# Transposes of the row maxima moved behind the first quarter of the late out-product, in a cross-attention and FFN block

## Chip, core and metric
The kernel runs on one core of one Trainium2 chip. The metric is the device time of one execution in microseconds (us). An execution has five engines that run their own instruction streams and meet by semaphores: TensorE (PE, with PEld for its weight loads), VectorE (DVE), ScalarE (ACT), GpSimd (POOL) and SyncE (SP), which issues the DMAs.

## What is computed
x is 4 x 2048 rows of 512, the context 4 x 154 rows of 512. Both residual branches have a layer norm ahead of them.

```python
x = x + _L0_xattn_ref(_layernorm(x), ctx, ctx, Wq, Wk, Wv, Wo, lam, g)
x = x + _L0_ffn_ref(_layernorm(x), ln1_g, ln1_b, w1, b1, ln2_g, ln2_b, w2, b2)
# attention: 16 heads of 32, two sets of queries and keys, 8 key heads
w1 = softmax(q1 @ k1.T); w2 = softmax(q2 @ k2.T)
attn = (w1 - lam * w2) @ v                     # then RMS norm, scale g, @ Wo.T
# ffn: 512 -> 2048 -> 512, weights quantised to -1, 0, 1 times a step
h = gelu(layer_norm(x, ln1_g, ln1_b) @ w1q.T + b1)
out = layer_norm(h, ln2_g, ln2_b) @ w2q.T + b2
```

## The kernel before, in words
The 8192 rows are cut into 16 blocks of 512 (`NBLK`), each of four groups of 128 rows (`tt`, 0 to 3). Weights, their transposes and the keys of the context are made once, in `setup` and `PROLOGUE`. Products in near-float32 precision are made of two or three float16 products of a high and a low part.

Every engine has a function `iteration(i)`, and the order of the work is written out by hand. There is no planner. The list `ATTEND` gives the first part of a block for all engines as words: `s` scores, `v` values, `q` a query product of the next block, `a` a piece of the attention result, and for the block before `e`, `f`, `h`, `i` parts of its late out-product, `g` the sums over its gelus, `y` and `z` the additions that finish its rows.

```python
ATTEND = [... "e2 g f2 y0 y1 s0 q0 z0 z1 y2 s1 v0 s2 h3 v1 ..." ...]
```

A block has these stages. In the first part (`ATTEND`) PE makes scores and values for block i, and finishes what the block before left. Then come the output projection (`out_projection`, L1173 to L1175 called with woT), the RMS sums, the rest of the queries, and a chain over DVE, ACT and POOL (`normalise`, `mid_rows`, layer norm) until PE transposes the normalised rows (`h_transposes`, L1315). The last stage is the FFN: 16 steps j. In each step PE makes the hidden product (`hidden`, L1325), scores of block i+1 in rows (`row_scores`, L1225), of which DVE takes the maxima (`row_max`, L890), and the out-product of the groups 0 and 1 three steps behind (`ffn_step`, L1347, PSUM banks 2 and 3). ACT makes gelu (L680, L683, L685), DVE the low part (`gelu_lo`, L987), and POOL sums the gelus and their squares (`sum_gelu`, L526). The out-product of the groups 2 and 3 is "late": it is made in the next block by `ffn_late` (L1337), group 2 in bank 5, as `e2` (four of 16 steps, eight matmuls) and `f2` (twelve steps, 24 matmuls), with `g` (`gelu_sums`, L1358, into bank 4) between them.

The row maxima of block i+1 are needed as two more rows of the operand `stack`, from which the scores of that block are made. When the last of 44 maxima is taken, DVE splits them (`split_maxima`, L897, L898, L900, semaphore `negmax_lo`), PE transposes them in four transposes into bank 6 (`transpose_maxima`, L1232, `negmax_transposed`), DVE copies them to SBUF (`copy_maxima`, L906), and SP brings them to `stack` in two DMAs (`stack_maxima`, L433, `negmax_stacked`). The first scores of a block (`scores`, L1250) write banks 0 to 3 and wait for three things around the change:

```python
wait(pe, s_nmst, c, 32, 32)        # the two DMAs of the maxima
wait(pe, s_gln, c - 1, 1, 1)       # L1001, which read the sums in bank 4
wait(pe, s_y, c - 1, TT, 2)        # y0, y1: add_ffn has read banks 2 and 3
```

`y0` and `y1` are `add_ffn` (L1013) on DVE. They need the scale of the layer norm over the gelus: `gelu_norm` on DVE (L994, L996, L998, L1001), a power on POOL (`power`, L483), then L1003 and L1005 on DVE. On POOL the four additions of a constant (`add_constant`, L513) stand ahead of that power, and they follow the last `sum_gelu`.

Of the kernel before, what the change touches and what calls it, by code (L numbers as in the profile page):

```python
# [91 lines left out]
def maxima_beside(j):  # L92

    first = sum(MAXIMA_AT[:j])
    return list(range(first, first + MAXIMA_AT[j]))


def wait(eng, sem, c, per, k):

    if isinstance(c, int) and c * per + k <= 0:  # L100
        return
    eng.wait_ge(sem, c * per + k)


def build(nc, x, ctx, wq, wk, wv, wo, lam, g, ln1_g, ln1_b, w1, b1, ln2_g, ln2_b, w2, b2, out):
# [7 lines left out]
    with ExitStack() as es:  # L113
# [17 lines left out]
        def ffn_bank(tt):  # L131

            return 2 + tt if tt < 2 else B_Q
# [950 lines left out]
        def _(pe):  # L1084
# [144 lines left out]
            def transpose_maxima(c):  # L1229
                wait(pe, s_nmlo, c, 1, 1)  # L1230
                for tt in range(TT):
                    ins = pe.transpose(ps[:, B_O, 0:TB // 2].bitcast(F16)[:, tt * P:(tt + 1) * P],  # L1232
                                       negmax16[:, tt, :, :].rearrange("p e u -> p (e u)"), ident16[:])
                ins.then_inc(s_nmt, 1)

            def scores(c, gi):


                if gi == 0:
                    wait(pe, s_nmst, c, 32, 32)  # L1240
                    if c:
                        wait(pe, s_gln, c - 1, 1, 1)
                        wait(pe, s_y, c - 1, TT, 2)
                    if c < NBLK - 1:
                        wait(pe, s_xt_lo, c + 1, TT, TT)
                else:
                    wait(pe, s_p, c, 2 * QM, 2 * gi)
                for i in range(UPT):
                    u = UPT * gi + i
                    ins = pe.matmul(ps[:, i, :], k_att[0:STKM, key_unit(u), 0:P], stack[0:STKM, u, :], start=True, stop=True)  # L1250
                    if i == 1:
                        ins.then_inc(s_s, 1)
                for i in range(UPT):
                    u = UPT * gi + i
                    ins = pe.matmul(ps[DH * i:DH * i + DH, B_SREST, :], k_att[0:STKM, key_unit(u), P:SPAD],  # L1255
                                    stack[0:STKM, u, :], start=True, stop=True)
                ins.then_inc(s_s, 1)

            def values(c, gi):

                m, buf = ORDER[gi] % (QM // 2), gi % 2
                b_o, b_l = value_banks(gi)
                wait(pe, s_p, c, 2 * QM, 2 * gi + 2)
                if gi == 0:
                    pe.wait_ge(s_vatt, 16 * (c // BLK_PER_BATCH + 1))
                elif gi % 2 and gi < QM - 1:
                    wait(pe, s_ol1, c, KD, gi // 2 + 1)
                else:
                    wait(pe, s_o2, c, KD, gi // 2)
                for i in range(UPT):  # L1270
                    kv = (UPT * m + i) // (H // KV)
                    pe.matmul(ps[DH * i:DH * i + DH, b_o, :], v_att[:, kv * DH:(kv + 1) * DH], probs[:, buf, i, :],  # L1272
                              start=True, stop=False)
                if gi % 2 == 0 and gi > 0:
                    wait(pe, s_ol2, c, KD, gi // 2)
                if gi == 0 and c < NBLK - 1:
                    wait(pe, s_q32, c + 1, QM, 1)
                for i in range(UPT):
                    pe.matmul(ps[DH * i:DH * i + DH, b_l, :], ones[:, 0:DH], probs[:, buf, i, :], start=True, stop=False)  # L1279

                wait(pe, s_r_lo, c, QM, gi + 1)
                v_hi, v_lo = (v_att[:, VM:].bitcast(F16).rearrange("p (h n) -> p h n", h=2)[:, h, m * P:(m + 1) * P]
                              for h in range(2))
                split_product(ps[:, b_o, :], v_hi, v_lo, p16[:, buf, 0, :], p16[:, buf, 1, :], False, True)
                pe.matmul(ps[:, b_l, :], ones_rest[:], p16[:, buf, 0, :], start=False, stop=False)
                pe.matmul(ps[:, b_l, :], ones_rest[:], p16[:, buf, 1, :], start=False, stop=True).then_inc(s_pv, 1)
# [9 lines left out]
            def out_projection(c, tt, pairs):  # L1296

                wait(pe, s_att_lo, c, KD, pairs[-1] + 1)
                cols = slice(tt * P, (tt + 1) * P)
                for k in pairs:  # L1300
                    ins = split_product(ps[:, tt, :], attn16[:, 0, k, cols], attn16[:, 1, k, cols], woT_hi[:, k, :],
                                        woT_lo[:, k, :], k == 0, k == KD - 1)
                if pairs[-1] == KD - 1:
                    ins.then_inc(s_wo, 1)
# [24 lines left out]
            def ffn_late(c, tt, js):  # L1329

                for j in js:
                    if j == 0 and tt == 2:
                        wait(pe, s_gelu, c, JH, JH)
                    elif j == 0:
                        wait(pe, s_y, c, TT, tt)
                    for e in range(2):
                        ins = pe.matmul(ps[:, ffn_bank(tt), :], gg16[:, j, e, tt * P:(tt + 1) * P], w2T[:, j, :],  # L1337
                                        start=(j == 0 and e == 0), stop=(j == JH - 1 and e == 1))
                if js[-1] == JH - 1:
                    ins.then_inc(s_f2, 1)  # L1340
# [11 lines left out]
            def gelu_sums(c):  # L1352

                wait(pe, s_acc, c, JH - 1, JH - 1)
                wait(pe, s_gelu, c, JH, JH - 1)
                for e in range(2):
                    for tt in range(TT):
                        ins = pe.matmul(ps[:, B_H, e * TT + tt:e * TT + tt + 1], acc[:, e, tt * P:(tt + 1) * P],  # L1358
                                        ones[:, 0:1], start=True, stop=True)
                ins.then_inc(s_sums, 1)  # L1360

            def iteration(i):
                ahead, ahead2 = i < NBLK - 1, i < NBLK - 2
                for what, n in ATTEND:
                    if what == "s":
                        scores(i, n)
                    elif what == "v":
                        values(i, n)
                    elif what == "e" and i:
                        ffn_late(i - 1, n, range(JH // 4))  # L1370
                    elif what == "f" and i:
                        ffn_late(i - 1, n, range(JH // 4, JH))
                    elif what == "h" and i:
                        ffn_late(i - 1, n, range(JH // 2))
                    elif what == "i" and i:
                        ffn_late(i - 1, n, range(JH // 2, JH))
                    elif what == "g" and i:
                        gelu_sums(i - 1)
                    elif what == "q" and ahead:
                        queries(i + 1, n)  # L1380
                for tt in range(TT):
                    if tt == TT - 1:
                        wait(pe, s_ol2, i, KD, KD)
                    out_projection(i, tt, (0, 1, 2))
                out_projection(i, 0, (3,))
                out_projection(i, 1, (3,))
                rms_sums(i)
                out_projection(i, 2, (3,))
                out_projection(i, 3, (3,))
                if ahead:  # L1390
                    for n in range(QATT, QEARLY):
                        queries(i + 1, n)
                h_transposes(i)
                if ahead:
                    for n in range(QEARLY, QM):
                        queries(i + 1, n)
                banks = (2, 3) if ahead else range(TT)
                for j in range(JH):
                    beside = maxima_beside(j) if ahead else []
                    hidden(i, j)  # L1400
                    for tb in beside[:2]:
                        row_scores(i + 1, tb)
                    if j >= FLAG:
                        ffn_step(i, j - FLAG, banks)
                    for tb in beside[2:]:
                        row_scores(i + 1, tb)
                    if ahead2 and j in XT_AT:
                        x_transposes(i + 2, XT_AT[j])
                for j in range(JH - FLAG, JH):
                    ffn_step(i, j, banks)  # L1410
                if ahead:
                    transpose_maxima(i + 1)

            setup()
            for what, n in PROLOGUE:
# [50 lines left out]
```

## Time and profile before

| | |
|---|---|
| median of 3 runs | 2459.5 us (2456.2 to 2461.03) |
| the profiled execution | 2460.22 us |
| its span, first to last instruction | 2456.9 us |
| mean granted clock of TensorE | 0.973 |
| busy: PE, DVE, ACT, POOL | 2301.5, 1719.6, 1339.5, 1012.2 us |

The profile is one execution. All places in time are us from the start of its span. Engine names with a q are their sequencers (SPq issues DMAs). Matmuls are pipelined: one of 512 columns is shown 0.38 us long, while the next may start after 0.22. "Idle before" is counted from the modelled end of the last one. A releaser is the instruction whose semaphore ended the wait.

### The profile page before, as it was taken

To read this page: it belongs to the slowest core of one execution; us is meant where nothing else is said; L and a number is where in the kernel's file an instruction comes from. 1 tells how busy PE (TensorE), PEld (TensorE's weight loads), DVE (VectorE), ACT (ScalarE), POOL (GpSimd) and SP (SyncE) were. 2 spreads that over 40 slices of the span, in tenths; PEclk is the share of its full clock that TensorE was granted. 3 is DMA by queue.
4 is the path that set the end of the run, shared out by engine and by line. 5 is a ranking of instruction groups with operands and counts; after the bars stand their busy time and mean duration, and the time that the engine had idled before them with its cause. 6 is when DMAs were issued, how large, how long until landed. Compare 5 with 4: busy or idle time off the path is not lost.

```text
span 2456.9 us, 35564 instructions
## 1 busy us (share of the span) xinstructions
PE 2301.5 (94%) x13663; PEld 1082.5 (44%) x13663; DVE 1719.6 (70%) x2714; ACT 1339.5 (55%) x1943; POOL 1012.2 (41%) x823
## 2 busy tenths in 40 slices
PE   8488999999999999999999999999999999999978
PEld 5243444535344453535444353534445353544433
DVE  3865858678585868768586776858586785857563
ACT  3325555546555555556555555655555465555544
POOL 0220543617153452716345271625436172534517
PEclk9688999999999999999999999999999999999989
DMA  6220203021130302111030202103030211202000
GB/s 256 74 77 11 69 15 89 13 69 26 37 84 15 90 15 68 25 60 44 23 97 15 78 15 69 36 23 82 15 101 19 65 27 33 72 15 74 15 22 17
DMA packets 105643, 125.85 MB, mean 51 GB/s; under 512 B 22496, under 2 KB 74268, under 8 KB 104964
## 3 DMA queue, kind: packets, MB, share of 16 engines
q1 hardware_dynamic: 105476, 123.60, 17.4%
q8 instruction: 108, 1.77, 0.3%
q14 instruction: 59, 0.48, 0.1%
HBM read 51.80 MB, written 20.36 MB: 29 GB/s over the span
## 4 chain that ended last, share of the span: by engine, by line
PE 69%; DVE 19%; issue 3%; ACT 3%; POOL 3%; DMA 2%; SPq 1%; POOLq 0%; ACTq 0%; DVEq 0%
PE ps L1325 16%; PE ps L1337 9%; PE ps L1347 7%; PE ps L1272 5%; PE ps L1225 5%; PE ps L1250 4%; PE ps L1173 4%; PE ps L1279 4%; PE ps L1174 3%; PE ps L1175 3%; DVE attn_raw L928 2%; DVE arena L987 2%; DVE arena L876 2%; DVE arena L890 2%; PE ps L1255 2%
## 5 line engine op out<-in xcount | busy, mean ns | idle before, releaser
L526 POOL TENSOR_TENSOR attn_raw<-attn_raw 128x512 f32<-128x512 f32 x448 | 580.2, 1314 | 146.5 <-ACT attn_raw L685 138.7
L1325 PE MATMUL ps<-rows,w1T 128*128 128x512 f16 x2048 | 485.5, 380 | 24.1 <-DVE rows L982 24.1
L890 DVE TENSOR_REDUCE arena<-ps 128x3 f32<-128x462 f32 (+1 forms) x704 | 413.8, 619 | 96.5 <-PE ps L1225 95.4
L494 POOL TENSOR_TENSOR q<-q 128x512 f16<-128x512 f32 x128 | 155.9, 1222 | 695.3 <-ACT q L631 678.5
L680 ACT ACTIVATE attn_raw<-ps,vec_cols,wstep 128x512 f32<-128x512 f32 x256 | 198.6, 776 | 267.0 <-PE ps L1325 265.2
L987 DVE SCALAR_TENSOR_TENSOR arena<-attn_raw,vec_cols,arena 128x512 f16<-128x512 f32 x256 | 233.1, 911 | 84.7 <-ACT arena L683 83.2
L1325 PEld LDWEIGHTS ps<-rows,w1T 128*128 128x128 f16 x2048 | 191.0, 97 | 220.7 <-DVE rows L982 37.2
L651 ACT ACTIVATE arena<-ps 128x1024 f32<-128x1024 f32 x128 | 131.6, 1028 | 266.6 <-PE ps L1250 266.6
L1347 PE MATMUL ps<-w2T,arena 128*128 128x512 f16 x1088 | 271.1, 379 | 0.0
L910 DVE SCALAR_TENSOR_TENSOR p<-arena,p 128x512 f16<-128x512 f32 x128 | 88.1, 689 | 254.4 <-ACT p L655 254.4
L1225 PE MATMUL ps<-k_att,stack_raw 96*128 96x154 f16 x2048 | 223.2, 234 | 23.1 <-DVE arena L890 21.6
L1225 PEld LDWEIGHTS ps<-k_att,stack_raw 96*128 96x128 f16 x2048 | 164.2, 98 | 144.4 <-DVE arena L890 66.4
L1337 PE MATMUL ps<-w2T,arena 128*128 128x512 f16 x960 | 217.3, 379 | 0.0
L928 DVE RECIPROCAL attn_raw<-attn_raw 128x512 f32<-128x512 f32 x64 | 214.1, 3346 | 0.0
L1173 PE MATMUL ps<-arena,wqT_hi 128*128 128x512 f16 x512 | 197.9, 387 | 4.7 <-DVE arena L951 4.2
L1174 PE MATMUL ps<-arena,wqT_hi 128*128 128x512 f16 x512 | 197.2, 385 | 0.0
L1175 PE MATMUL ps<-arena,wqT_lo 128*128 128x512 f16 x512 | 196.7, 384 | 0.0
L683 ACT ACTIVATE arena<-attn_raw,vec_cols 128x512 f16<-128x512 f32 x256 | 184.8, 722 | 8.3
L653 ACT ACTIVATE arena<-ps 128x1536 f32<-128x1536 f32 x128 | 186.2, 1455 | 0.4 <-PE ps L1255 0.4
L629 ACT ACTIVATE q<-ps 128x512 f32<-128x512 f32 x128 | 76.4, 596 | 200.8 <-PE ps L1175 180.8
L685 ACT ACTIVATE attn_raw<-attn_raw 128x512 f32<-128x512 f32 x256 | 156.9, 613 | 0.0
L1272 PE MATMUL ps<-arena,v_att 128*32 128x512 f32 x1024 | 136.7, 606 | 2.2 <-ACT arena L651 1.1
(164 smaller groups left out, 3436.5 us busy)
## 6 DMA issues: line engine op xcount, KB each, us to landing
stack_raw<-q SPq DMA_DIRECT2D x768, 64.0 KB, 2.0
arena<-in_x SPq DMA_DIRECT2D x16, 1024.0 KB, 6.2
arena<-in_x SPq DMA_DIRECT2D x64, 256.0 KB, 2.6
out<-arena SPq DMA_DIRECT2D x64, 256.0 KB, 2.0
arena<-in_L_ffn_w SPq DMA_DIRECT2D x8, 1024.0 KB, 10.5
stack_raw<-in_L_xattn_Wq SPq DMA_DIRECT2D x8, 256.0 KB, 10.8
k_att<-k_store SPq DMA_DIRECT2D x4, 490.0 KB
k_store<-attn_raw SPq DMA_DIRECT2D x12, 160.0 KB
```

The lines of the kernel that those rows point to most:

```text
L526: ins = pool.tensor_tensor(acc[:, e, :], acc[:, e, :], src[:, j % NG, :], ALU.add)
L890: dve.tensor_reduce(negmax[:, tt, u0:u1], ps[:, row_bank(c, tb), 0:(u1 - u0) * S].rearrange("p (u s) -> p u s", s=S), AX.X, ALU.max, negat ...
L928: dve.reciprocal(l_prod, l_prod).then_inc(s_inv, 1)
L987: dve.scalar_tensor_tensor(gg16[:, j, 1, :], gelu_t[:, j % NG, :], g2_col[:, j:j + 1], gg16[:, j, 0, :], ALU.mult, ALU.subtract).then_inc( ...
L1173: pe.matmul(dst, w_hi, r_hi, start=first, stop=False)
L1174: pe.matmul(dst, w_hi, r_lo, start=False, stop=False)
L1175: return pe.matmul(dst, w_lo, r_hi, start=False, stop=last)
L1225: ins = pe.matmul(ps[:, row_bank(c, tb), w * S:(w + 1) * S], stack[0:STK, u, tt * P:(tt + 1) * P], k_att[0:STK, key_unit(u), 0:S], start=T ...
L1272: pe.matmul(ps[DH * i:DH * i + DH, b_o, :], v_att[:, kv * DH:(kv + 1) * DH], probs[:, buf, i, :], start=True, stop=False)
L1325: ins = pe.matmul(ps[:, B_H + j % 2, :], w1T[:, k, j * P:(j + 1) * P], rows16[:, e, k, :], start=(k == 0 and e == 0), stop=(k == KD - 1 an ...
L1337: ins = pe.matmul(ps[:, ffn_bank(tt), :], gg16[:, j, e, tt * P:(tt + 1) * P], w2T[:, j, :], start=(j == 0 and e == 0), stop=(j == JH - 1 a ...
L1347: ins = pe.matmul(ps[:, bank, :], gg16[:, j, e, tt * P:(tt + 1) * P], w2T[:, j, :], start=(j == 0 and e == 0), stop=(j == JH - 1 and e == 1))
```

## The change
In `iteration(i)` of PE the call of `transpose_maxima` moves from the end of the block, where it stood for block i+1, to the next block, behind the word `e`. There it is called for block i itself. The call for block 0, ahead of the loop, stays.

```diff
                     elif what == "e" and i:
                         ffn_late(i - 1, n, range(JH // 4))
+                        transpose_maxima(i)
                     elif what == "f" and i:
...
                 for j in range(JH - FLAG, JH):
                     ffn_step(i, j, banks)
-                if ahead:
-                    transpose_maxima(i + 1)
```

On PE the seam between two blocks then reads differently. This is one of the 15 seams, which are all alike. Words in brackets are the semaphores that the instruction waits for (`gelu` the activation, `gelu_summed` POOL's sums, `gelu_lo` DVE's low part).

Before:

```order
L1347 MATMUL ps<-w2T,arena 128x512 x3
L1232 MATMUL ps<-ident,arena 128x128 [waits negmax_lo]
L1232 MATMUL ps<-ident,arena 128x128 x3
L1337 MATMUL ps<-w2T,arena 128x512 [waits gelu]
L1337 MATMUL ps<-w2T,arena 128x512 x7
L1358 MATMUL ps<-ones,attn_raw 128x1 [waits gelu,gelu_summed]
L1358 MATMUL ps<-ones,attn_raw 128x1 x7
L1337 MATMUL ps<-w2T,arena 128x512 x24
L1250 MATMUL ps<-stack_raw,k_att 128x512 [waits ffn_out_read,x_lo,gelu_ln_step,negmax_stacked]
```

With the change:

```order
L1347 MATMUL ps<-w2T,arena 128x512 x3
L1337 MATMUL ps<-w2T,arena 128x512 [waits gelu]
L1337 MATMUL ps<-w2T,arena 128x512 x7
L1232 MATMUL ps<-ident,arena 128x128 [waits negmax_lo]
L1232 MATMUL ps<-ident,arena 128x128 x3
L1358 MATMUL ps<-ones,attn_raw 128x1 [waits gelu,gelu_summed]
L1358 MATMUL ps<-ones,attn_raw 128x1 x7
L1337 MATMUL ps<-w2T,arena 128x512 x24
L1250 MATMUL ps<-stack_raw,k_att 128x512 [waits ffn_out_read,x_lo,gelu_ln_step,negmax_stacked]
```

The four transposes and the eight matmuls of the quarter have changed places, and everything around them stands as before. DVE's part of the seam is the same in both:

```order
L900 SCALAR_TENSOR_TENSOR arena<-arena 128x4x32 [waits negmax_hi]
L906 COPY sq_acc<-ps 64x512 [waits negmax_stacked,negmax_transposed]
L994 TENSOR_SCALAR mean_g<-ps 128x4 [waits gelu_sums]
L996 TENSOR_TENSOR meansq_g<-mean_g 128x4 [waits gelu_ln_small_step]
L998 SCALAR_TENSOR_TENSOR var_g<-ps,meansq_g 128x4 [waits gelu_ln_small_step]
L1001 TENSOR_SCALAR var<-var_g 128x4 [waits gelu_ln_small_step]
L1003 TENSOR_SCALAR scale_g<-rstd,wstep 128x4 [waits gelu_rstd]
L1005 SCALAR_TENSOR_TENSOR shift_g<-mean_g,scale_g 128x4 [waits gelu_ln_small_step]
L1013 SCALAR_TENSOR_TENSOR arena<-ps,scale_g,arena 128x512 [waits gelu_ln_small_step,const_added,ffn_out]
```

Nothing moved here, nor on SP, ACT and POOL; L906 waits for the transposes that moved on PE.

## Rows read from the trace of the kernel before

**Rows 1.** The page: PE's busy time, and the chain that ended last by engine.
```profile
PE 2301.5 (94%) x13663; PEld 1082.5 (44%) x13663; DVE 1719.6 (70%) x2714; ACT 1339.5 (55%) x1943; POOL 1012.2 (41%) x823
...
PE 69%; DVE 19%; issue 3%; ACT 3%; POOL 3%; DMA 2%; SPq 1%; POOLq 0%; ACTq 0%; DVEq 0%
```

**Rows 2.** Waits of PE, 290 to 2300: us in total, times, longest.
```profile
PE ps L1325 <- DVE rows L982: 20.3, 14, 1.6
PE ps L1232 <- DVE arena L900: 14.7, 14, 1.1
```

**Rows 3.** Chain of waits across one seam, 465 to 486: start, us, what.
```profile
466.94 0.79 ACT attn_raw L680
...
471.81 0.40 PE ps L1232 x4
```

**Rows 4.** Timeline of PE at that seam: start, us, what, idle before it.
```profile
468.01 2.75 PE L1347 MATMUL ps<-w2T,arena 128*128 128x512 f16 x12
471.81 0.40 PE L1232 MATMUL ps<-ident,arena 128*128 128x128 f16 x4 [1.05 <-DVE arena L900]
472.05 1.89 PE L1337 MATMUL ps<-w2T,arena 128*128 128x512 f16 x8
473.77 1.84 PE L1358 MATMUL ps<-ones,attn_raw 128*128 128x1 f32 x16
475.48 5.34 PE L1337 MATMUL ps<-w2T,arena 128*128 128x512 f16 x24
480.65 1.03 PE L1250 MATMUL ps<-stack_raw,k_att 98*128 98x512 f16 x4
```

**Rows 5.** Chain of waits in the middle of a block, 526 to 562.
```profile
532.38 0.23 PE ps L1286
...
558.14 1.92 PE ps L1325 x8
```

**Rows 6.** Weight loads: one group of the page, and the timeline at the seam.
```profile
L1325 PEld LDWEIGHTS ps<-rows,w1T 128*128 128x128 f16 x2048 | 191.0, 97 | 220.7 <-DVE rows L982 37.2
...
475.37 4.95 PEld L1337 LDWEIGHTS ps<-w2T,arena 128*128 128x128 f16 x24
```

**Rows 7.** Timeline of DVE at the seam.
```profile
470.50 1.25 DVE L900 SCALAR_TENSOR_TENSOR arena<-arena 128x128 f16<-128x128 f32 x1
472.25 0.42 DVE L906 COPY sq_acc<-ps 64x512 f16<-64x512 f16 x1 [0.49 <-PE ps L1232]
475.65 0.16 DVE L994 TENSOR_SCALAR mean_g<-ps 128x4 f32<-128x4 f32 x1 [2.99 <-PE ps L1358]
...
478.49 1.41 DVE L1013 SCALAR_TENSOR_TENSOR arena<-ps,scale_g,arena 128x512 f32<-128x512 f32 x2
```

**Rows 8.** Timeline of POOL at the seam.
```profile
469.07 2.54 POOL L526 TENSOR_TENSOR attn_raw<-attn_raw 128x512 f32<-128x512 f32 x2 [0.59 <-ACT attn_raw L685]
471.56 4.98 POOL L513 TENSOR_TENSOR arena<-arena,out_const 128x512 f32<-128x512 f32 x4
477.05 1.02 POOL L483 TENSOR_TENSOR rstd<-var,neghalf 128x4 f32<-128x4 f32 x1 [0.50 <-DVE var L1001]
```

**Rows 9.** Timeline of POOL in mid-block: two powers in a row.
```profile
543.88 2.00 POOL L483 TENSOR_TENSOR rstd<-var,neghalf 128x4 f32<-128x4 f32 x2 [2.00 <-DVE var L942]
```

**Rows 10.** SP's two DMAs at the seam, and the landing of all 32.
```profile
472.69 1.20 SPq L433 DMA_DIRECT2D stack_raw<-sq_acc  x2
...
DMA to landing us min/median/max: 2.7/3.3/3.7
```

**Rows 11.** Busy us (and instructions) by stretch: PE, PEld, DVE, ACT, POOL, PEclk, DMA, GB/s.
```profile
330.00:470.70 140.70, 136.64 (x821) 63.63 (x820) 102.22 (x159) 80.84 (x116) 61.89 (x51) 1.00 0.17 46
...
689.85:693.26 3.41, 3.38 (x9) 1.17 (x10) 3.33 (x9) 0.31 (x1) 1.11 (x2) 0.50 0.45 108
```

**Rows 12.** Timeline of PE in block 3, a query product.
```profile
689.88 0.59 PE L1173 MATMUL ps<-arena,wqT_hi 128*128 128x512 f16 x1 [2.24 <-DVE arena L951]
...
693.25 0.39 PE L1175 MATMUL ps<-arena,wqT_lo 128*128 128x512 f16 x1
```

## The prediction
> **What bounds the kernel now.** I read the engine shares on the page, then TensorE's waits in the steady part, then the chain of waits, and last the timelines of every engine around one seam between two blocks. PE is busy 94% of the span, and the chain that ended last lies on PE for 69% and on DVE for 19% [rows 1]. So a wait of PE is paid in full unless something else is just as late. In the steady part the two longest waits of PE [rows 2] are L1325, after the projection's layer norm, and L1232, the transposes of this change: 14.7 us in 14 places, never over 1.1 us. The chain of waits across the seam [rows 3] goes back from the transposes to the last gelu on ACT. It is a latency chain of ACT and DVE that PE waits out.
>
> The timelines of the seam between blocks 1 and 2 [rows 4] give the size. Late out-product matmuls start 0.216 us apart (24 of them last 5.34 with the last taking 0.38: 4.96 / 23). The last matmul of the early out-product starts at 468.01 + 2.75 - 0.38 = 470.38, so PE could issue the next at 470.60. It issues the first transpose at 471.81, released by DVE's L900 of 470.50 + 1.25 = 471.75. **The hole is 471.81 - 470.60 = 1.21 us**; the view calls 1.05 of it idle, because it counts from a modelled end. The hole stands in front of each of 15 transposes in the loop. In the other 14 seams the distance from L900 to L1232 looks the same, since the longest of these waits is 1.1.
>
> Everything else in a block hangs on PE. In the middle of a block the chain leaves PE's last value product (L1286), runs over DVE, ACT and POOL, and comes back to PE at L1325 [rows 5]. It starts from PE and has no fixed time of its own. What PE gains at the seam should therefore stay gained to the end.
>
> **The change, step by step.** It adds and removes nothing: four transposes move past the eight matmuls of `ffn_late(i - 1, 2, first quarter)` on PE. The instructions of DVE, SP, POOL and ACT keep their order, so no queue but PE's is passed.
>
> 1. The quarter moves up. It waits for the last gelu, which ends at 466.94 + 0.79 = 467.73 [rows 3], 2.9 us before 470.60. It starts at 470.60 and takes 473.77 - 472.05 = 1.72 [rows 4], until 472.32. Cost nothing; it fills the hole.
> 2. The transposes now come up at 472.32. Their data is there at 471.75 [rows 7], and 0.06 later PE was released before, so the wait is covered with 0.51 us to spare. They take 472.05 - 471.81 = 0.24. PE goes on at 472.56. If the cover were gone (data over 0.5 us later), the rest of the wait would simply come back.
> 3. The weight load of the first transpose now stands behind a running matmul. A load takes 97 ns, and the 24 loads of the late product lie within 4.95 us beside 24 matmuls 0.216 us apart [rows 6], so a load of this size hides. I take 0, upper bound 0.10 per seam. The Trainium skill's page "TensorE: Matmul & The Clock Gate" (Part 3, The mechanism) says that a weight load overlaps running matmuls only when it goes to another row group. The late product's loads and matmuls use the same 128 rows, so by that rule each pair would stand 0.31 us apart; the trace disagrees.
> 4. The sums (`gelu_sums`, L1358) come at 472.56 instead of 473.77, 1.21 earlier. They wait for POOL's last sum of gelus, which ends at 469.07 + 2.54 = 471.61 [rows 8]: 0.95 us to spare. The 24 matmuls behind them are issued 1.21 earlier too. PE is ready for the scores (L1250) at 480.65 - 1.21 = 479.44.
> 5. The scores wait for two things that do not move by 1.21, and here the change can lose.
>    - **The second `add_ffn`** (L1013), which frees the last of the banks that the scores write, ended at 478.49 + 1.41 = 479.90 [rows 7], 0.75 before the scores. Its chain starts with the sums: L994 to L1001 on DVE, the power on POOL, L1003, L1005, two L1013. DVE's part moves by 1.21: L1001, which released the power at 477.05, now could at 475.84. But POOL is in its four additions until 471.56 + 4.98 = 476.54, and these do not move. So the power starts at 476.54 and not at 477.05 [rows 8], 0.51 earlier, and L1013 ends at 479.39. A release of 0.05 or 0.06 behind that makes 479.45, against PE's 479.44. I take 0.01 us lost. Whether POOL starts the power right behind an addition is not seen at this place; where two powers follow each other they last 2.00 us together against 1.02 for one [rows 9], which leaves no pause. Bounds: the chain moves by 0.55 (nothing lost), or not at all (scores at 479.95, 0.51 lost).
>    - **The maxima's copy and DMA.** DVE's copy L906 follows the transposes, from 472.25 to 472.77. SP issues two DMAs in a row (1.20 us together), landing at most 3.7 us after issue [rows 10]. Before, SP started 0.02 after the copy, so now at 473.21; the second issue is at about 473.82 and lands by 477.5. That is 1.9 us ahead of 479.44. Cost nothing. DVE's copy also stands ahead of L994, which starts at 474.4 at the earliest; the copy ends at 473.2.
>
> Sum: 15 seams x 1.21 = 18.2 us gained, 15 x 0.01 = 0.2 lost, 18.0 net. The profiled execution took 2460.2 us (span 2456.9 and 3.3 around it), the median of the runs is 2459.5, 0.7 lower. So 2442.2 for an execution like the profiled one, and **2441.5 for the median**. That is 0.73%, where a measurement of this kernel can tell about 0.2% (4.9 us) from no change.
>
> **Rivals.**
> (a) *POOL and the add hold the scores.* The hole is closed but a part of it opens again in front of L1250, because POOL's power comes late behind the additions, or because L1013 is slower beside them. At worst the scores stand at 479.95: 1.21 - 0.51 = 0.70 per seam, 10.5 us, 2449.0. For it: the margin is only 0.01 us. Against it: POOL shows no pause between operations. Chance 0.09.
> (b) *The moved loads do not hide.* One load of 0.10 exposed per seam: 1.5 us less gain, 2443.0. The rows against it are in step 3. This is what the quoted rule of the Trainium skill would do here. Chance 0.02.
> (c) *The maxima land late.* The copy ends 0.52 later and the scores are wanted 1.21 earlier, so slack shrinks by 1.73. If a DMA needed twice its time (6.6 instead of 3.3), it would land at 480.4, the scores would start 0.2 earlier than before, and the time would be 2457, no change that can be told. Against it: 3.7 is the longest of 32 landings [rows 10], and nothing else uses the queue then. Chance 0.04.
> (d) *The clock, slower than before.* PE's clock is at its full level (1.00, 2.4 GHz) through the ordinary blocks, and at 0.50 (1.2 GHz) in a stretch of block 3 [rows 11]. That stretch begins where PE had stood idle for 2.24 us in front of a query product [rows 12], and there eight matmuls stood 0.42 instead of 0.216 us apart, which costs 1.6 us. PE also idles 1.5 us in front of L1325 in each block. If the new spacing of blocks made the clock fall there each time, it would cost 15 x 1.6 = 24.7 us, 6.5 more than the gain: 2466. It turns the sign from 11 blocks on. Against it: the 1.05 us of idle time that goes stood in stretches at 1.00, and less idle time is no reason for a lower clock. A dip more or less (1.6 us) is likely enough and belongs to the range. Chance 0.03.
> That the change does not do what it says is excluded by the order of PE's instructions.
>
> **How the numbers follow.** My forecast has 0.82, (a) 0.09, (b) 0.02, (c) 0.04, (d) 0.03. The forecast, (a) and (b) are faster: 0.93; (c) is no change: 0.04; (d) is slower: 0.03. The low end takes the lowest run before, 2456.2, less the full 18.2: 2438.0. The high end is the bound of (a), 2449.0. (c) and (d) are left out, with the tails of the rest.
>
> **What would show it.** In the new profile the seam should read, on PE: L1347, L1337 x8, L1232, L1358 without idle time between them, and L1232 gone from the waits. From L1347's last start to L1250's first there should be 9.06 us instead of 10.27 in all 15 seams. POOL's power should follow the additions at once, with DVE as no releaser, and L1250 should have next to no wait. The ordinary block should take about 139.5 us instead of 140.7 (the length of the first stretch in [rows 11]). It would be wrong if L1250 showed a wait on L1013 of over 0.2 us (rival a), if a gap opened at L1232's load (b), if L1250 waited for the DMA (c), or if the granted clock fell in many blocks (d), and wrong in its premise if PE's seam were 1.2 us shorter and the block as long as before.

## The result, and the profile after

| | before | changed |
|---|---|---|
| first comparison, median | 2460.01 us (4 runs) | 2443.55 us (4 runs, 2443.25 to 2449.02) |
| second comparison, median | 2459.1 us (9 runs) | 2446.17 us (5 runs, 2443.27 to 2448.67) |
| profiled execution, span | 2456.9 us | 2446.6 us |

The change makes the kernel faster. The ratio was 0.9941 (95% interval 0.9924 to 0.9959) the first time and 0.9945 (0.9932 to 0.9959) the second. That is 10 to 19 us and 10 to 17 us. I had forecast 18.0 us, 2441.5 us.

One execution differs from another by several us for reasons outside the change (shown further down). The seams are a sharper measure, because the ordinary block repeats to a few hundredths. It took 140.7 us before [rows 11]. In the changed kernel a stretch of 139.77 us holds the same 821 matmuls (columns as there):

```profile
471.00:610.77 139.77, 136.66 (x821) 63.63 (x820) 102.97 (x158) 80.85 (x116) 61.89 (x51) 1.00 0.17 46
```

So a seam gives 0.92 us (140.69 from one L900 to the next before, 139.77 now) and 15 seams give 13.8 us. The forecast was 1.20 per seam.

Waits of PE from 290 to 2300 us in the changed kernel (us in total, times, longest):

```profile
PE ps L1325 <- DVE rows L982: 20.5, 14, 1.9
PE ps L1225 <- DVE arena L890: 13.2, 28, 0.6
...
PE ps L1250 <- issue: 0.4, 2, 0.2
```

The transposes' wait (L1232, 14.7 us in [rows 2]) is gone and the others stand as before. PE's timeline at the same seam answers to [rows 4]:

```profile
467.13 2.75 PE L1347 MATMUL ps<-w2T,arena 128*128 128x512 f16 x12
469.72 1.89 PE L1337 MATMUL ps<-w2T,arena 128*128 128x512 f16 x8
471.45 0.39 PE L1232 MATMUL ps<-ident,arena 128*128 128x128 f16 x4
471.67 1.90 PE L1358 MATMUL ps<-ones,attn_raw 128*128 128x1 f32 x16
473.43 5.34 PE L1337 MATMUL ps<-w2T,arena 128*128 128x512 f16 x24
478.87 1.02 PE L1250 MATMUL ps<-stack_raw,k_att 98*128 98x512 f16 x4
```

I count from the start of the last L1347 matmul, 467.13 + 2.75 - 0.38 = 469.50. The hole in front of the transposes has closed. The last late matmul starts at 473.43 + 5.34 - 0.38 = 478.39, so PE could take the scores at 478.61, 9.11 behind the mark. L1250 starts at 478.87, 9.37 behind it; before it was 10.27. A new hole of 0.26 us has opened, too short for the view to print as idle. DVE and POOL at the seam, answering to [rows 7] and [rows 8]:

```profile
473.61 0.16 DVE L994 TENSOR_SCALAR mean_g<-ps 128x4 f32<-128x4 f32 x1 [1.32 <-PE ps L1358]
473.80 0.66 DVE L996 TENSOR_TENSOR meansq_g<-mean_g 128x4 f32<-128x4 f32 x1
474.50 0.16 DVE L998 SCALAR_TENSOR_TENSOR var_g<-ps,meansq_g 128x4 f32<-128x4 f32 x1
474.69 1.00 DVE L1001 TENSOR_SCALAR var<-var_g 128x4 f32<-128x4 f32 x1
...
477.20 1.41 DVE L1013 SCALAR_TENSOR_TENSOR arena<-ps,scale_g,arena 128x512 f32<-128x512 f32 x2
```

```profile
470.69 4.97 POOL L513 TENSOR_TENSOR arena<-arena,out_const 128x512 f32<-128x512 f32 x4
475.77 1.02 POOL L483 TENSOR_TENSOR rstd<-var,neghalf 128x4 f32<-128x4 f32 x1
```

Two of the rows that [rows 7] leaves out, from the same timeline of the kernel before:

```profile
475.85 0.72 DVE L996 TENSOR_TENSOR meansq_g<-mean_g 128x4 f32<-128x4 f32 x1
...
476.80 0.17 DVE L1001 TENSOR_SCALAR var<-var_g 128x4 f32<-128x4 f32 x1
```

L1001 works on four numbers per partition. It took 0.17 us before and now takes 1.00. It ends at 475.69, 0.03 behind the end of POOL's four additions (475.66). `add_ffn` (L1013) ends at 477.20 + 1.41 = 478.61, and L1250 follows 0.26 behind that.

**The rest of the profiled execution.** Its time, 2449.02 us, is 5.5 above the other three runs of the first comparison. DVE's timeline in block 4 shows one cause:

```profile
822.17 2.47 DVE L861 BATCH_NORM_STATS2 stats<-arena 128x6 f32<-128x512 f32 x4 [2.06 <-DMA arena<-in_x]
```

The 1 MB load of x landed 10.0 us after its issue there and 9.8 in block 10; the median of the loads is 6.2. Those two blocks took 141.93 and 141.72 us instead of 139.77. The order of the loads did not change, and the second profile of the changed kernel has 139.78 us in block 4 and 139.79 in block 10. So this is scatter that the change did not bring. (A third load, in block 11, took 9.97 us; there PE's granted clock also stood at 0.50 for 3.4 us, from 1812.9 on, behind 2.15 us of idle time in front of a query product.)

The mean granted clock goes with the scatter between executions. Of the 39 executions of the kernel before that stood beside the experiments, 16 had 0.973 or 0.974 (median 2461.7 us) and 8 had 0.977 or more (2457.6 us). Of the nine executions of the changed kernel, five had 0.973 or 0.974 (2446.4 us) and four 0.977 or more (2443.4 us); three of these four stand in the first comparison. At like clocks the difference is 15.2 and 14.2 us. One difference of the clock lies in the setup, which the change does not touch. From 17.5 to 27.7 us the clock stood at 0.50 in the profile of the changed kernel and at 1.00 in that of experiment 1, though PE had the same 19 matmuls in both.

### The profile page after: what moved, and what is told of

The parts are those of the page before. It is cut to its first block, busy times and chain, and to the rows that moved or that the text cites. A ratio compares the mean times of both kernels' runs of the same rounds, so it can differ in the third digit from the quotient of the medians.

```text
span 2446.6 us, 35564 instructions
## 1 busy us (share of the span) xinstructions
PE 2303.2 (94%) x13663; PEld 1082.0 (44%) x13663; DVE 1731.0 (71%) x2714; ACT 1340.0 (55%) x1943; POOL 1011.9 (41%) x823
## 4 chain that ended last, share of the span: by engine, by line
PE 70%; DVE 17%; issue 3%; DMA 3%; POOL 3%; ACT 2%; SPq 1%; POOLq 0%; ACTq 0%; DVEq 0%
PE ps L1325 16%; PE ps L1347 9%; PE ps L1337 9%; PE ps L1225 5%; PE ps L1272 5%; PE ps L1250 4%; PE ps L1173 4%; PE ps L1279 4%; PE ps L1174 3%; PE ps L1175 3%; DVE attn_raw L928 2%; DVE arena L987 2%; DVE arena L876 2%; PE ps L1255 2%; DMA arena<-in_x 2%
## 5 line engine op out<-in xcount | busy, mean ns | idle before, releaser
L987 DVE SCALAR_TENSOR_TENSOR arena<-attn_raw,vec_cols,arena 128x512 f16<-128x512 f32 x256 | 233.2, 911 | 85.1 <-ACT arena L683 83.5
L1347 PE MATMUL ps<-w2T,arena 128*128 128x512 f16 x1088 | 271.1, 379 | 0.0
L1337 PEld LDWEIGHTS ps<-w2T,arena 128*128 128x128 f16 x960 | 91.6, 99 | 109.5 <-issue 6.8
## 6 DMA issues: line engine op xcount, KB each, us to landing
arena<-in_L_ffn_w SPq DMA_DIRECT2D x8, 1024.0 KB, 10.6
```

The costliest lines, as they stand in the source:

```text
L987: dve.scalar_tensor_tensor(gg16[:, j, 1, :], gelu_t[:, j % NG, :], g2_col[:, j:j + 1], gg16[:, j, 0, :], ALU.mult, ALU.subtract).then_inc( ...
L1347: ins = pe.matmul(ps[:, bank, :], gg16[:, j, e, tt * P:(tt + 1) * P], w2T[:, j, :], start=(j == 0 and e == 0), stop=(j == JH - 1 and e == 1))
```

## The experiments

Theory A, formed from the new profile, has two parts. POOL's running additions hold back two small DVE operations and the power, so `add_ffn` still ends late. And since it is now the last thing the scores wait for, PE's restart behind it costs more than the 0.05 us that I had read from the transposes' release.

**1. The wait for `add_ffn` as the last of the four.** In the built program, the wait written first comes last.

```diff
                 if gi == 0:
-                    wait(pe, s_nmst, c, 32, 32)
                     if c:
-                        wait(pe, s_gln, c - 1, 1, 1)
                         wait(pe, s_y, c - 1, TT, 2)
+                        wait(pe, s_gln, c - 1, 1, 1)
+                    wait(pe, s_nmst, c, 32, 32)
```

> The changed kernel with the four waits of the first scores in another order, so that the wait for add_ffn (L1013) is the last that PE's sequencer takes and not the first. Theory A (the scores are released late by L1013, and the sequencer then works off two more waits, 0.11 us each): L1250 starts some 0.05 us behind the end of L1013 instead of 0.26, the ordinary block takes 139.57 instead of 139.77 us, and the time is 3 us below the changed kernel's 2443.5, about 2440.5. Rival R (a restart of PE costs this much whatever the order of the waits): L1250 0.26 behind L1013, 139.77, 2443.5.

Measured: 2442.35 us against 2459.28, ratio 0.9935 (0.9922 to 0.9947); ordinary block 139.60. DVE and PE at the seam:

```profile
474.73 1.41 DVE L1013 SCALAR_TENSOR_TENSOR arena<-ps,scale_g,arena 128x512 f32<-128x512 f32 x2
```

```profile
476.20 1.04 PE L1250 MATMUL ps<-stack_raw,k_att 98*128 98x512 f16 x4
```

L1013 ends at 476.14 and L1250 starts 0.06 behind it. In the changed kernel the same distance is 0.26, and the trace's semaphore records there show the sequencer taking up the wait for L1013 at 478.65 and the next at 478.76, 0.11 later, although what that one waited for had long come. Behind the late wait the sequencer takes up two more steps, one with two semaphores (of x and of L1001) and one, at the weight load of L1250, for the maxima. In experiment 1 the late wait is the one at that weight load. In all 15 seams L1250 starts 0.06 behind L1013 there. So 0.17 us per block, 2.6 us in all, is what the two steps behind the late one cost. The whole times agree with it (1.2 us between medians of different comparisons) but could not show it alone.

**2. Two of POOL's additions held back.** `add_ffn` needs the constant only for groups 0 and 1 here.

```diff
                     if what == "g" and i:
-                        add_constant(i - 1, range(TT))
+                        add_constant(i - 1, range(TT // 2))
                         power(3, s_gln, s_rstd4, i - 1)
+                        wait(pool, s_y, i - 1, TT, 2)
+                        add_constant(i - 1, range(TT // 2, TT))
```

> The changed kernel, with two of POOL's four additions of the constant behind its power, and held there until the second add_ffn is done. Theory A (L1001 on DVE cannot work beside POOL's additions, which thereby hold the power, add_ffn and the scores): L996 and L1001 take under 0.25 us each instead of 0.66 and 1.00, L1013 ends some 1.3 us earlier, L1250 follows the late product without idle time, 9.11 instead of 9.37 us behind the last matmul of L1347; the block takes 139.51 and the time is 3.9 us below the changed kernel, about 2439.6. Rival (the DVE operations are slow by themselves, or L1250 waits for the DMA of the maxima): L1250 stays 9.37 behind, 2443.5.

Measured: 2440.38 us against 2459.28, ratio 0.9926 (0.9914 to 0.9939); ordinary block 139.52. Lines stand two higher here: L998 is L996 of before, L1003 is L1001, L1015 is L1013. DVE at the seam:

```profile
471.62 0.16 DVE L998 TENSOR_TENSOR meansq_g<-mean_g 128x4 f32<-128x4 f32 x1
...
472.02 0.17 DVE L1003 TENSOR_SCALAR var<-var_g 128x4 f32<-128x4 f32 x1
...
473.70 1.41 DVE L1015 SCALAR_TENSOR_TENSOR arena<-ps,scale_g,arena 128x512 f32<-128x512 f32 x2
```

and PE:

```profile
464.95 2.75 PE L1349 MATMUL ps<-w2T,arena 128*128 128x512 f16 x12
...
476.43 1.03 PE L1252 MATMUL ps<-stack_raw,k_att 98*128 98x512 f16 x4
```

With POOL idle, both operations take 0.16 and 0.17 us. `add_ffn` ends at 475.11, 1.3 us ahead of the scores, and these start 476.43 - 467.32 = 9.11 behind the mark, as expected. The seam now gives 1.17 instead of 0.92 us.

**3. The same edit on the kernel before.**

> The kernel before, with the same edit on POOL. There PE is released by nothing at L1250 and L1013 ends 0.75 us ahead of it. Theory A: L1013 ends over 1 us earlier and nothing is gained, the block stays at 140.69 and the time at 2460, within 2 us. Rival (POOL's additions cost time in themselves, by slowing DVE or PE elsewhere): as much gained as in the run of the changed kernel with this edit, 4 us or so.

Measured: 2458.36 us against 2459.28, ratio 1.0 (0.9991 to 1.001); ordinary block 140.68. `add_ffn` ends 1.32 us ahead of the scores instead of 0.76, which is less than the gain of over 1 us that I expected, and nobody waits for it. POOL's additions cost time only once the change has made the scores depend on them.

**4. Two additions right behind the power, not held.** As in 2, without the `wait` on `s_y`.

> The changed kernel, with two of the four additions directly behind the power, and not held. Theory A (a DVE operation with two operands in SBUF, or one that works from SBUF to SBUF with a scalar, has to let POOL's running addition end): L1003 waits for the third addition and L1005 for the fourth, add_ffn ends some 0.8 us later than in the changed kernel, L1250 too, and the gain shrinks by about 12 us: 2455 or so. Rival (POOL is merely late because its queue is full): the power starts 1.3 us earlier and add_ffn with it, 2439.6.

Measured: 2456.24 us against 2459.28, ratio 0.9988 (0.9979 to 0.9997); ordinary block 140.43. Lines stand one higher. POOL, then DVE, then PE:

```profile
475.59 1.02 POOL L483 TENSOR_TENSOR rstd<-var,neghalf 128x4 f32<-128x4 f32 x1 [1.22 <-DVE var L1002]
476.58 2.48 POOL L513 TENSOR_TENSOR arena<-arena,out_const 128x512 f32<-128x512 f32 x2
```

```profile
476.64 1.23 DVE L1004 TENSOR_SCALAR scale_g<-rstd,wstep 128x4 f32<-128x4 f32 x1 [1.13 <-POOL rstd L483]
477.91 1.18 DVE L1006 SCALAR_TENSOR_TENSOR shift_g<-mean_g,scale_g 128x4 f32<-128x4 f32 x1
479.01 1.40 DVE L1014 SCALAR_TENSOR_TENSOR arena<-ps,scale_g,arena 128x512 f32<-128x512 f32 x2
```

```profile
480.66 1.02 PE L1251 MATMUL ps<-stack_raw,k_att 98*128 98x512 f16 x4 [0.75 <-DVE arena L1014]
```

The next two DVE operations, 0.23 and 0.16 us by themselves, take 1.23 and 1.18. Each lasts to the end of one of POOL's additions. The scores wait 0.75 us by the view, and most of the gain is lost (0.26 us per block is left of 0.92). This is what rival (a) of the prediction describes, and past its bound: the scores start 10.01 us behind the mark, where (a) had 479.95 - 470.38 = 9.57 at worst. The Trainium skill names the sharing in "GPSIMD Engine Reference" (Specifications): the SBUF interfaces are shared with VectorE, with contention for DVE instructions that have two SBUF inputs or run in a two-port mode. The trace agrees as far as it goes: L996 and L1005, which were held, have two SBUF inputs, and L994 and L998, which read PSUM, took 0.14 to 0.16 in all runs. L1001 and L1003 go from SBUF to SBUF with one tensor input; whether they ran in such a mode is not in the trace.

**5. Half of the cover.** Four of the eight matmuls ahead of the transposes, four behind.

```diff
-                        ffn_late(i - 1, n, range(JH // 4))
+                        ffn_late(i - 1, n, range(JH // 8))
                         transpose_maxima(i)
+                        ffn_late(i - 1, n, range(JH // 8, JH // 4))
```

> The changed kernel with four of the quarter's eight matmuls ahead of the transposes and four behind. They are 0.86 us of cover for a hole of 1.21: 0.35 stays in front of the transposes. Theory A (the gain is the smaller of what the cover gives and what add_ffn behind POOL's additions allows): PE is ready for the scores 9.11 + 0.35 = 9.46 us behind the last matmul of L1347, add_ffn was released at 9.11 and is no longer waited for; the block takes 139.86, 1.4 us in all above the changed kernel: 2445. Rival (the gain comes from all of the cover, and the scores' delay is a cost of the transposes' new place): L1250 0.26 later still, 140.1, 2449.

Measured: 2449.36 us against 2459.98, ratio 0.9955 (0.9943 to 0.9968); ordinary block 139.83. PE:

```profile
469.40 0.40 PE L1232 MATMUL ps<-ident,arena 128*128 128x128 f16 x4 [0.19 <-DVE arena L900]
```

Part of the hole is back in front of the transposes, as it should be with 0.86 us of cover. The block is only 0.06 longer than with the full quarter, because what is lost here was lost at the scores there. The scores start 9.41 behind the mark, where I expected 9.46, and `add_ffn` ended 0.29 ahead of them. The median lies 4.4 us above the expected 2445. Against its own kernel before it is 10.6 us lower (8 to 14), where the seams give 15 x 0.86 = 12.9, so the interval holds what the seams say.

**6. The transposes behind the sums.** `transpose_maxima(i)` moves on, behind `gelu_sums(i - 1)`.

> The changed kernel with the transposes behind the sums (L1358) too. The sums come 0.22 us earlier and the maxima 1.7 us later. Theory A (POOL's additions hold L1001 and so the power, whenever the sums are ready): L1001 still ends with the fourth addition, L1250 starts where it did or 0.05 us earlier, the maxima land at most 0.5 us ahead of it; 139.77 or 139.75, 2443.5. Rival C (the maxima's DMA takes over as the last wait): L1250 is released by the DMA of L433, the block takes over 140, above 2447.

Measured: 2447.45 us against 2459.98, ratio 0.9947 (0.9934 to 0.9961); ordinary block 139.79. L1001 took 1.00 us again and ended with the fourth addition; the maxima landed at 476.88, 0.9 ahead of the scores (477.82), where I expected 0.5 at most. The transposes can be another 1.7 us late without a cost, so rival (c) was far off: the second DMA lands 3.3 us after its issue, as before.

**7. All four additions in mid-block.** `add_constant(i, range(TT))` stands behind the last `q_lo` of a block and ahead of its first `sum_gelu`.

> The changed kernel with POOL's four additions in the block that they belong to, behind its last query part and ahead of its first sum of gelus. Theory A: at the seam the same as with two additions ahead: L996 and L1001 under 0.25 us, L1250 without a wait, 0.26 us per block gained. But the additions now run beside the first steps of the FFN, where DVE's L987 has two operands in SBUF and POOL's sums start 0.4 us late; I expect 0.3 to 1.0 us per block lost there, 2444 to 2454. Rival (POOL disturbs DVE only at the seam): 2439.6.

Measured: 2473.36 us against 2459.98, ratio 1.0057 (1.0043 to 1.007). The seam is as expected, 9.11 us and L1001 (here L1000) at 0.17, but most blocks take 140.9 or 142.6. Of the ten ordinary ones four take 140.9, five 142.6, and one, which waits 1.9 us for a load of x, 142.5. Lines stand one lower. The loss is larger than I expected and its cause another. L987 did not get slower (mean 904 ns against 911). The first part of the loss is 1.4 us per block, from 139.5 to 140.9. POOL's row shows the additions in front of the first sum of gelus:

```profile
560.22 5.93 POOL L513 TENSOR_TENSOR arena<-arena,out_const 128x512 f32<-128x512 f32 x4
566.11 2.94 POOL L522 TENSOR_TENSOR attn_raw<-attn_raw 128x512 f32<-128x512 f32 x2
569.20 7.06 POOL L526 TENSOR_TENSOR attn_raw<-attn_raw 128x512 f32<-128x512 f32 x5
```

and of ACT's waits one is new (its gelu, 14 times, up to 3.4 us), and of PE's one has grown from 13.2 us:

```profile
ACT attn_raw L679 <- issue: 33.4, 14, 3.4
```

```profile
PE ps L1224 <- DVE arena L889: 36.2, 25, 3.2
```

By the code, a gelu waits for the sum three steps behind it, and POOL had no room left at the start of the FFN. That this is the whole of the first part was read from these rows, not tested.

The second part is 1.7 us in each of the five blocks of 142.6. One of them, one of 140.9, and a stretch of the first (columns as in [rows 11]; the third column from the end is the granted clock):

```profile
472.31:614.94 142.63, 138.19 (x822) 64.25 (x820) 101.53 (x159) 80.75 (x117) 62.97 (x51) 0.99 0.17 45
901.84:1042.78 140.94, 136.50 (x822) 63.67 (x820) 101.51 (x158) 80.73 (x117) 62.97 (x51) 1.00 0.17 46
573.90:577.30 3.40, 3.40 (x12) 1.46 (x11) 1.79 (x2) 0.00 (x0) 3.26 (x3) 0.51 0.00 0
```

All five have such a stretch of 3.4 us at 0.50, and none of the other five blocks has one. That is what rival (d) of the prediction describes, brought by this edit and not by the change. In the first of the five PE had idled 2.00 us in front of L1224 (until 572.84) before the clock fell. In the block of 140.94 it idled 2.00 us at the same place (until 1002.37) and the clock stayed at 1.00, so this idle time alone does not tell which blocks have such a stretch.

**8. The two edits of 6 and 2 together.**

> Transposes behind the sums, and two of POOL's additions held back until the second add_ffn is done. Theory A: the sums start 0.22 us earlier and are 0.05 shorter when they follow the out-product and not the transposes; add_ffn has 1 us of slack; the maxima land 0.5 to 0.9 us ahead of the scores. The block takes 139.46 to 139.52, the time is 2438.8 to 2439.6, at or just under the kernel with the additions held back alone. Rival C: the DMA of the maxima is last, and the block takes over 139.8.

Measured: 2441.16 us against 2459.98, ratio 0.9928 (0.9915 to 0.994); ordinary block 139.46. PE:

```profile
471.82 1.84 PE L1360 MATMUL ps<-ones,attn_raw 128*128 128x1 f32 x16
473.52 0.38 PE L1234 MATMUL ps<-ident,arena 128*128 128x128 f16 x4
473.74 5.34 PE L1339 MATMUL ps<-w2T,arena 128*128 128x512 f16 x24
```

The sums take 1.70 us to the next start where they follow the late product, against 1.76 behind the transposes (473.43 - 471.67 in the changed kernel). It is the shortest block of all, 1.23 us below the kernel before. The median lies above the 2438.8 to 2439.6 that I expected. By whole times this kernel cannot be told from experiment 2.

**9 and 10. The changed kernel and experiment 2 again, on one chip.**

> The changed kernel itself once more, since its first comparison had an interval from 10 to 19 us. If the seams are all that changed, the gain is 15 x 0.92 = 13.8 us (the ordinary block 139.77 against 140.69): about 2446. If there is another gain of some us elsewhere in the block, 2443.5 comes again.

> The changed kernel with two of POOL's additions held back, once more and on the same chip as the changed kernel. Theory A: 15 x 0.25 = 3.8 us below it, and 15 x 1.17 = 17.6 us below the kernel before: about 2442. Rival: no difference to the changed kernel.

Measured: 2446.17 and 2443.79 us against 2459.1, ratios 0.9945 (0.9932 to 0.9959) and 0.9938 (0.9925 to 0.995); ordinary blocks 139.78 and 139.51. The first comparison's 16.5 us was a little high; 12.9 here, beside 13.8 by the seams. The two variants differ by 2.4 us in whole time, where the seams say 3.8 to 4. The sign is the same in both comparisons, but the intervals overlap; only the block length shows it clearly. The versions with additions held back beat both kernels of this study by that measure.

## Why the prediction was right, and where it was off

**The premise held.** The hole was 1.21 us, it hung on DVE's L900, and PE's later work follows PE. In all variants the gain per block was what PE gained at the seam. The time lies in the range and the direction is right. That the first comparison came within 2 us of the forecast is luck in part: it shows 16.5 us, where the seams give 13.8 and the forecast was 18.0.

**Steps 1 to 3 held.** The quarter starts at 469.72, 0.22 behind the mark, and lasts 1.73. The transposes follow without a wait. Their weight load hides: they follow 1.73 us behind the start of eight matmuls. Rival (b) fell.

**What the hole was made of.** I took it for a chain of ACT and DVE that PE has to wait out. In fact POOL stretches it. At every seam L898 takes 0.65 us and L900 1.25 ([rows 7] for L900), beside POOL's last sum of gelus, and L900 ends 0.14 us behind that sum (471.75 and 471.61). Ahead of the first block POOL is idle. There, in the kernel before, L898 takes 0.16 us and L900 0.29:

```profile
198.25 0.29 DVE L900 SCALAR_TENSOR_TENSOR arena<-arena 128x128 f16<-128x128 f32 x1
```

All twelve traces show the same pair of values. By an estimate from these rows, the two operations would be done 0.49 + 0.96 = 1.45 us earlier with POOL out of the way, which is more than the hole of 1.21. No experiment moved POOL's sums, so this is not tested.

**Step 4 was 0.05 us short per seam.** PE was ready for the scores 9.11 us behind the mark and not 9.06. The float32 sums need 1.76 us behind the transposes, 1.71 behind the late product [rows 4]; experiment 8 gives 1.70 there.

**Step 5 failed in two sizes.** The step said that POOL's additions would hold the power and then let `add_ffn` end 0.05 us ahead of the need, with 0.01 lost. In place of the sentence "DVE's part moves by 1.21", L1001 moved by 0.40 (6.59 behind the mark before, from the end of its 0.17, and 6.19 after), since it cannot finish beside an addition. The sum survived this for the most part, because the power had to wait for the same additions in any case: it started 6.27 behind the mark where I had 6.16, and `add_ffn` ended 9.11 behind where I had 9.01. The larger error is the sentence "a release of 0.05 or 0.06 behind that". I took that from a wait that stands alone (L900 to L1232). The scores have four waits, and with `add_ffn`'s taken up first the restart costs 0.26. So the scores started 9.37 and not 9.07 behind the mark: 0.05 for the sums, 0.05 for the later end, 0.20 for the waits. The experiments take these apart: 9.37 in the changed kernel, 9.18 with the late wait taken up last (1), 9.11 where `add_ffn` is no longer waited for (2). 15 x 0.30 = 4.5 us, of the 18.0 forecast 13.5, against 13.8 by the block lengths.

**Rival (a) was the place, in part.** I gave 0.09 to a part of the hole opening again in front of L1250, with 0.70 per seam as its low bound. It did open, by 0.26, and the seam gave 0.92. The forecast and this rival met in the middle, so the margin of 0.01 us should have had more weight. The contention was there to be seen in the trace before: L996 took 0.72 us for four numbers and ended at 476.57, with POOL's last addition (476.54 in [rows 8]).

**Rivals (c) and (d).** The maxima had 2.6 us to spare (landed at 476.24, scores at 478.87). The clock was at 1.00 in the ordinary block shown; its mean over the profiled execution was 0.973 both before and after, and each has one stretch of 3.4 us at 0.50 in its steady part (at 689.9 and at 1812.9).

## What to carry to other kernels

When a wait on the bound engine is filled with work, look up what the next join waits for and move every input of it by its own amount: an input that hangs on another engine's queue does not move along. A margin of hundredths of a microsecond at a join with several waits is not a margin. Put the wait that comes last where the engine takes it up last, and before giving a helper engine filler work, check whether small operations of its neighbour on the critical chain have to stand behind it. Look for that also in the wait that you mean to fill: compare the durations of its operations with the same operations at a place where the helper is idle.

## What was not expected of the hardware

- A DVE operation on 128 x 4 numbers (0.16 to 0.23 us by itself) takes up to 1.23 us when it falls into a POOL addition over 128 x 512 in SBUF: it ends within some 0.05 us of the end of the addition. Seen for L996, L1001, L1003 and L1005, not for the two that read PSUM. L898 and L900 on 128 x 128 numbers (0.16 and 0.29 us by themselves) take 0.65 and 1.25 beside POOL's sums of 128 x 512, and L900 ends 0.14 us behind the sum.
- Waits that are taken up behind the late one at the same PE instruction cost 0.2 us for two steps (three semaphores), though they had long been fulfilled. A late wait that is taken up last costs 0.06.
- A stretch of 3.4 us with the granted clock at 0.50 came in five of the ten ordinary blocks of experiment 7 and cost 1.7 us each time.
- The 16 float32 matmuls of one column took 0.05 us longer behind float16 transposes than behind float16 matmuls of 512 columns. Why was not tested.
